# Second layer's edge counts: parts visited in twos, both one-hots on VectorE, ScalarE left with copies

## The reference

```python
h = maximum(layernorm(x), 0)
x_hyp = expmap0(h)
gx = gamma * x_hyp
num = segment_sum(edge_weight[:, None] * gx[dst], src)   # and a denominator beside it
x = x + logmap0(0.5-scaled num / den)
```

## Time and profile before

| | |
|---|---|
| median of 3 runs | 4671.01 us (4664.2 to 4673.88) |
| the profiled execution, its own time | 4658.9 us |
| its span in the trace | 4657.2 us |
| busy in the span: PE, VectorE, ScalarE, POOL | 1625.0, 2841.6, 1721.5, 2023.8 us |
| `blend_and_count` in the trace | about 2100 to 2936 us |

### The profile page before, as it was taken

The page is one execution under the profiler, slowest core; times in us unless marked ns, Lnnn a source line. Parts: engine busy times, 40 slices in busy tenths (PEclk is TensorE's granted clock), DMA queues, the critical chain, the costliest instruction groups (busy, mean ns, idle before and its releaser), DMA issues. The chain is left out here.

```text
span 4657.2 us, 48027 instructions
## 1 busy us (share of the span) xinstructions
PE 1625.0 (35%) x10415; PEld 925.7 (20%) x10415; DVE 2841.6 (61%) x4999; ACT 1721.5 (37%) x4632; POOL 2023.8 (43%) x2740
## 2 busy tenths in 40 slices
PE   3152111100000000002454434222222179899989
PEld 2132111100000000000111101111121069444444
DVE  5837699774677789881354434738697857422131
ACT  1324312102565667331454444325454465111011
POOL 0065788727777710026456663067777540000000
PEclk6576555555555555555665555655555589999999
DMA  3000000016666610002122222168788545777846
GB/s 131 15 19 1 3 1 1 1 57 180 183 182 184 186 42 0 0 18 44 33 62 65 65 64 67 57 184 266 246 261 251 162 128 149 287 240 268 283 162 204
DMA packets 215402, 553.56 MB, mean 119 GB/s; under 512 B 46177, under 2 KB 112411, under 8 KB 214404
## 3 DMA queue, kind: packets, MB, share of 16 engines
q0 software_dynamic: 99984, 272.83, 21.3%
q1 hardware_dynamic: 115188, 278.18, 17.6%
HBM read 485.70 MB, written 65.20 MB: 118 GB/s over the span
## 5 line engine op out<-in xcount | busy, mean ns | idle before, releaser
L2913 PE MATMUL fourth_bank<-fourth_tile,fourth_z 128*128 128x512 f16 (+1 forms) x2800 | 557.2, 360 | 20.1 <-DVEq L3074 10.1
L2272 POOL DMA_INDIRECT heads_got<-rec,heads_slot x416 | 479.2, 1152 | 153.2 <-issue 94.4
L1372 POOL DMA_INDIRECT blend_got<-rec,blend_slot x416 | 403.7, 971 | 291.2 <-DVE second_sums L1412 163.1
L1793 POOL DMA_INDIRECT sum_got<-rec,sum_slot x416 | 440.9, 1060 | 158.7 <-issue 90.2
L1099 POOL DMA_INDIRECT table<-edges_record,edges_place x391 | 419.1, 1072 | 123.5 <-POOL table_pause L260 85.7
L1424 DVE TENSOR_SCALAR blend_mov<-built_iota_low,built_low 128x800 f16 x492 | 218.9, 445 | 377.6 <-issue 226.5
L1492 PE MATMUL blend_count<-blend_mov,blend_stat 128*128 x492 | 220.7, 449 | 459.0 <-issue 302.9
L214 PE MATMUL edges_p_key<-kept_ident,edges_key_row 128*128 128x128 f32 x4 | 1.1, 424 | 1013.6 <-DVEq L176 1013.6
L1879 DVE TENSOR_TENSOR first_y<-first_y,sum_got 128x516 f32 x416 | 291.4, 701 | 80.6 <-issue 34.5
L1465 ACT ACTIVATE blend_gap<-built_iota_ten,built_offset 128x128 f32 x492 | 197.2, 401 | 382.7 <-issue 252.5
L2386 DVE TENSOR_TENSOR third_a_y<-third_a_y,heads_got 128x520 f32 x416 | 288.0, 692 | 60.5 <-issue 36.4
(11 more groups left out here) (679 smaller groups left out, 4694.4 us busy)
## 6 DMA issues: line engine op xcount, KB each, us to landing
fourth_tile<-cs SPq DMA_DIRECT2D x100, 800.0 KB, 4.4
fourth_tile<-ct SPq DMA_DIRECT2D x100, 800.0 KB, 4.4
ct<-blend_cst SPq DMA_DIRECT2D x20, 1000.0 KB
heads_counts<-ct SPq DMA_DIRECT2D x25, 800.0 KB
cs<-heads_flipped SPq DMA_DIRECT2D x25, 800.0 KB
attend_cnt<-ct SPq DMA_DIRECT2D x50, 256.0 KB
sort_low_wide<-low SPq DMA_DIRECT2D x4, 3136.0 KB, 21.7
attend_cnt<-ct SPq DMA_DIRECT2D x25, 288.0 KB
```

The lines of the kernel that those rows point to most:

```text
L1372: pool.indirect_dma_start(got[:, t % KEPT, :], None, rec_dram, bass.IndirectOffsetOnAxis(ap=slot[:, t:t + 1], axis=0)).then_inc(gathered[p ...
L1793: pool.indirect_dma_start(got[:, t % (HELD * PART), :], None, rec_dram, bass.IndirectOffsetOnAxis(ap=slot[:, t:t + 1], axis=0)).then_inc(g ...
L2272: pool.indirect_dma_start(got[:, buf, r, :], None, rec_dram, bass.IndirectOffsetOnAxis(ap=slot[:, t:t + 1], axis=0)).then_inc(gathered[buf ...
L2913: last = pe.matmul(bank[m][:, 0:w], z2[s % 2][:, k, part, :], tile[:, n % RING, at:at + w], start=(k == 0 and part == 0), stop=(k == NB - ...
```

## The change

- The loops go over pairs of parts. `prepare_edges` makes the span of each block even and at least four parts: first part at most `ET - 4`, end rounded up so that the length is even. The tables are two parts longer so that a pair may reach past the last.
- VectorE makes both one-hots, for both parts of a pair: four TENSOR_SCALAR instructions (is_equal), the new ones 128 numbers wide, from 16-bit numbers against `K["offset"]`, which now holds the key minus the start of the group of ten blocks.
- ScalarE has no loop, registers, `gap` or steps for `stat`. It waits for a constant value of `block_done` and copies the block.
- TensorE waits once for a pair and has four matmuls in an iteration. Behind each block comes a matmul of zeros two columns wide that signals `block_done`.
- The rings hold 4 pairs in place of 8 parts.

```diff
-                step(dve.tensor_scalar(K["offset"][:, k, :], K["key"][:, 0:ET], -1.0, float(k * GROUP * P), ALU.mult, ALU.add))
+                step(dve.tensor_scalar(K["offset"][:, k, :], K["key"][:, 0:K["offset"].shape[2]], -float(k * GROUP * P), None, ALU.add))
...
-            step(dve.tensor_scalar(span[:, :, 0], first[:, :], float(ET - 2), None, ALU.min))
-            step(dve.scalar_tensor_tensor(last[:, :], span[:, :, 0], 1.0, last[:, :], ALU.add, ALU.max))
-            step(dve.tensor_scalar(span[:, :, 1], last[:, :], 1.0, None, ALU.add))
+            step(dve.tensor_scalar(span[:, :, 0], first[:, :], float(ET - 4), None, ALU.min))
+            step(dve.scalar_tensor_tensor(last[:, :], span[:, :, 0], 3.0, last[:, :], ALU.add, ALU.max))
+            step(dve.tensor_tensor(last[:, :], last[:, :], span[:, :, 0], ALU.subtract))
+            step(dve.tensor_scalar(last[:, :], last[:, :], 0.5, 0.75, ALU.mult, ALU.add))
+            step(dve.tensor_scalar(last[:, :], last[:, :], ROUND_MAGIC, -ROUND_MAGIC, ALU.add, ALU.add))
+            step(dve.scalar_tensor_tensor(span[:, :, 1], last[:, :], 2.0, span[:, :, 0], ALU.mult, ALU.add))
...
-    RING, BANKS = 8, 2
+    RING, BANKS = 4, 2
-    stat, mov = c.sb("stat", [P, RING, P], BF16), c.sb("mov", [P, RING, IL], BF16)
-    gap = c.sb("gap", [P, RING, P], BF16)
+    stat, mov = c.sb("stat", [P, RING, 2 * P], BF16), c.sb("mov", [P, RING, 2 * IL], BF16)
...
-                with dve.Fori(*tiles_of(dve, tiles, b)) as t:
+                ids = K["iota_ten"][:, b % GROUP * P:(b % GROUP + 1) * P]
+                first, end = tiles_of(dve, tiles, b)
+                with dve.Fori(first, end, step=2) as t:
                     n, at = slot_of(dve, made)
                     dve.wait_ge(slot_free, n + 1)
-                    dve.tensor_scalar(at_slot(mov, at), K["iota_low"][:, :], K["low"][:, bass.ds(t, 1)], None, ALU.is_equal).then_inc(mov_ready, 1)
+                    movs, stats = at_slot(mov, at), at_slot(stat, at)
+                    for k in range(2):
+                        done = dve.tensor_scalar(movs[:, k * IL:(k + 1) * IL], K["iota_low"][:, :], K["low"][:, bass.ds(t, 2)][:, k:k + 1], None, ALU.is_equal)
+                        done = dve.tensor_scalar(stats[:, k * P:(k + 1) * P], ids, K["offset"][:, b // GROUP, bass.ds(t, 2)][:, k:k + 1], None, ALU.is_equal)
+                    done.then_inc(slot_ready, 1)
                     dve.reg_add(made, made, 1)
...
-                act.wait_ge(slot_free, act.snap(visits[b % 2], min_val=1, max_val=BLOCKS * ET) + RING)
+                act.wait_ge(block_done, b + 1)
...
-                with act.Fori(*tiles_of(act, tiles, b)) as t:
-                    n, at = slot_of(act, matched)
-                    act.wait_ge(mov_ready, n + 1)
-                    act.activation(at_slot(gap, at), ids, ACT.Abs, bias=K["offset"][:, b // GROUP, bass.ds(t, 1)]).then_inc(gap_ready, 1)
-                    narrow_of_the_last(n)
-                    act.reg_add(matched, matched, 1)
+                take(b)
...
-                pe.wait_ge(stat_ready, n + 2)
-                pe.matmul(banks[0], at_slot(stat, at), moving[:, 0:IL // 2], start=first, stop=True, skip_group_check=True)
-                pe.matmul(banks[1], at_slot(stat, at), moving[:, IL // 2:IL], start=first, stop=True, skip_group_check=True).then_inc(slot_free, 1)
+                pe.wait_ge(slot_ready, n + 1)
+                movs, stats = at_slot(mov, at), at_slot(stat, at)
+                for k in range(2):
+                    for half in range(2):
+                        done = pe.matmul(banks[half], stats[:, k * P:(k + 1) * P], movs[:, k * IL + half * IL // 2:k * IL + (half + 1) * IL // 2],
+                                         start=first and k == 0, stop=True, skip_group_check=True)
+                done.then_inc(slot_free, 1)
...
-                with pe.Fori(first + 1, end):
+                with pe.Fori(first + 2, end, step=2):
                     visit(banks, False)
+                pe.matmul(banks[1][:, 0:2], K["zero"][:, 0:P], K["zero"][:, 0:2], start=False, stop=True, skip_group_check=True).then_inc(block_done, 1)
```

More of the change, by code:

```diff
@@ L236, in tiles_of @@
     first, end = regs[0][b % GROUP], regs[1][b % GROUP]
-    return eng.snap(first, min_val=0, max_val=ET - 1), eng.snap(end, min_val=1, max_val=ET)
+    return eng.snap(first, min_val=0, max_val=ET - 4), eng.snap(end, min_val=4, max_val=ET + 1)
 class Chain:
@@ L1343, in blend_and_count @@
     gathered = [c.gather_sem(f"gathered{k}") for k in range(PARTS_KEPT)]
-    mov_ready, gap_ready, stat_ready, slot_free = c.sem("mov_ready"), c.sem("gap_ready"), c.sem("stat_ready"), c.sem("slot_free")
+    slot_ready, slot_free, block_done = c.sem("slot_ready"), c.sem("slot_free"), c.sem("block_done")
     sum_free = c.sem("sum_free")
@@ L1433, in _ @@
         def _(act):
-            act.preload_act_table(ACT.Relu)
-            act.copy(at_slot(gap, RING - 1), K["zero"][:, 0:P]).then_inc(gap_ready, 1)
-            matched = counter(act, "matched")
-            visits = [counter(act, f"visits{k}") for k in range(2)]
-            tiles = range_registers(act)
             def take(b):
@@ L1489, in visit @@
                 n, at = slot_of(pe, used)
-                pe.wait_ge(stat_ready, n + 2)
-                moving = at_slot(mov, at)
-                pe.matmul(banks[0], at_slot(stat, at), moving[:, 0:IL // 2], start=first, stop=True, skip_group_check=True)
-                pe.matmul(banks[1], at_slot(stat, at), moving[:, IL // 2:IL], start=first, stop=True, skip_group_check=True).then_inc(slot_free, 1)
+                pe.wait_ge(slot_ready, n + 1)
[5 more added lines that the diff above has]
+                done.then_inc(slot_free, 1)
                 pe.reg_add(used, used, 1)
@@ L1602, in second_layer @@
             K.update(key=ci.sb("key", [P, 512]), low=ci.sb("low", [P, 512]), ones=ci.sb("ones", [P, P]),
-                     iota_low=ci.sb("iota_low", [P, IL], F16), iota_ten=ci.sb("iota_ten", [P, GROUP * P]),
-                     offset=ci.sb("offset", [P, BLOCKS // GROUP, ET]), range=ci.sb("range", [1, 512], I32))
+                     iota_low=ci.sb("iota_low", [P, IL], F16), iota_ten=ci.sb("iota_ten", [P, GROUP * P], F16),
+                     offset=ci.sb("offset", [P, BLOCKS // GROUP, ET + 2]), range=ci.sb("range", [1, 512], I32))
             prepare_edges(nc, src, dst, range_dram, K, h, gam, feat, sums, passed, rec_dram)
```

12 lines of the change are left out of this document (removed).

## The result

The changed kernel takes 4599.1 us (median of 4 runs, 4591.96 to 4614.23) against 4670.17 for the kernel before on the same chip (4 runs). The ratio is 0.9851, 95% interval 0.9816 to 0.9886: 71 us, or 1.5%, faster. The forecast was 4636 us, with a range from 4530 to 4685, which holds the result; the forecast's own range, 4600 to 4660, ends 1 us above it. The gain is twice the 35 us that were forecast.

A forecast was written before the change was run, and what follows sets the result against it. Beside gathers, the slowest engine's control instructions, about 0.7 us each, were taken as the bound. Terms -20, -20 and +9 gave -31, rounded to -35 us: 4636 beside the median 4671.0; range 4530 to 4685, own range 4600 to 4660.

The forecast's parts named there:

- The first stretch: From the first compare to the first add in `blend_and_count`: TensorE sets the pace, first add at 2273 us, -20 us.
- The price forecast: TensorE beside the gathers, before the first add: each control instruction costs 0.71 us, so a pair takes 5.7 us.
- The middle: Blocks while adds and gathers mix, 2302 to 2854 us: VectorE takes 8.5 us a block beside gathers, not 9.1; -20 us.
- the rule: Beside the gathers, the slowest engine's control-instruction count sets the pace; in the middle VectorE's 29 a block take 9.1 us.
- the bound named for TensorE alone: Middle: if TensorE's 21 control instructions for 28 set the pace, 6.8 us a block, 61 blocks fit, -72 us.
- The undisturbed block: A middle block while no gathers run: 4.8 us, from 3.6 + 1.4 x 0.92.
- The last blocks: The last 23 blocks, with no gathers: 4.0 us each against 3.6, +9 us.
- The narrow compare: VectorE's new 128-wide compare: 200 ns each, two in a pair of 1.2 us.
- no term: POOL's gathers: disturbance of only 9 us and more idle time than that, so nothing in the sum.
- That the slots go: Beside the gathers, the 0.7 us slots vanish or shrink as ScalarE leaves: 4425 to 4485 us, half relief 4550; chance 0.17.
- that VectorE's sequencer becomes the bound: Beside the gathers, ten or more control instructions a pair make the kernel slower: +38 us, 4709; chance 0.17.
- No change: Whole stage: 12% more parts eat the shorter loops' gain; start -15, middle -5, end +15, 4666 us; chance 0.12.

The follow-up runs named there:

- the kernel that it is measured against: The changed kernel with POOL waiting for the adds before every gather in place of every eighth: 4547.61 us, ratio 0.9846.

## Why the forecast fell short

**The first stretch.** The forecast was the first add at 2273 us (-20); in the first profile it starts at 2266.3 (-28). That the number is so near is in part luck, for in other profiles of the same instructions the first add follows the first gather 31 to 64 us sooner. The mechanism was as told: near 700 ns for TensorE's address steps, while VectorE's stay short:

```profile
L1431 DVEq FUSED_REGOPS  x24: 16/120/158, 2163.4 to 2235.0; - x24
```

The count was eight control instructions on TensorE and seven on VectorE, as forecast. The price forecast, 8 x 0.71 = 5.7 us a pair, is what the steady part has; the mean of the 80 us is 6.15. From 2120 to 2256 us there are 29 pairs (58 narrow compares) where 24 were expected, since the slow instructions set in gradually: 14 of the 29 pairs fall in the first 43 us. The prediction says that all three engines are busy for under a fifth of this stretch; TensorE's 28.61 us of 136 are 21%, which changes nothing in the argument.

**The middle is the step that failed.** The prediction put it at -20: "if VectorE, now alone, does a block in 8.5, 49 blocks fit beside the gathers", which is -15, and 5 more "since TensorE's wait for ScalarE goes too". It is -43. By the prediction's own division, 521 us less 418 us of gathers are 103, at 4.8 us 21.5 blocks, and the other 56.5 of the 78 took 7.4 us each, not 8.5.

What stood behind the 8.5 was that VectorE's own count stays at 29 a block and sets the pace, and that ScalarE's leaving "frees the chain of jitter, but not VectorE's own count". The count did stay, so the whole -20 was the price of what ScalarE's leaving frees, and this term was too small. Two runs show it. With ScalarE out and single parts VectorE has 34 control instructions a block; by the rule the middle would be some 30 us longer (9.1 x 34 / 29 = 10.7 us a block), and the kernel is 22 us faster. From pairs with ScalarE in to the changed kernel the count goes up from 24 to 29; by the rule the middle would be some 45 us longer, and the kernel is 24 us faster. Taken together ScalarE's leaving is worth an estimated 50 to 70 us beside the gathers, out of which VectorE's added count is paid.

VectorE's count does matter in the middle, as told: two more a pair cost 26 us there and 47 in all. TensorE's doesn't show in the middle (2 us); its 26 us are to be looked for in the first stretch, where the first add comes 33 us later behind the first gather than in the kernel that it is measured against (160.5 us, 127 there), part of which is the scatter of that stretch. So the bound named for TensorE alone (6.8 us, 61 blocks) is nearer to the measured 7.4 than the value taken, but not for its reason. Why ScalarE's loop cost so much is open. It isn't a loop of control instructions on its sequencer (+8 us, inside the intervals), and a relay through it costs some 13 us. ScalarE's activations in the loop are what is left, and they were not tested by themselves. How the 67 us divide between the first stretch and the middle rests on one profile of each kernel; the whole, -71 and -70 us on two chips, doesn't.

The undisturbed block near 4.8 us held: without gathers the adds take 447 us before and 453 after. (Its working, 3.6 + 1.4 x 0.92, is 4.9, and the difference is too small to matter.) But it held as a sum of two things that the prediction didn't name: pairs shorten it (430 us with ScalarE in) and VectorE's extra compares lengthen it.

**The last blocks.** The forecast was +9 us; it is +2. The narrow compare is slower than forecast:

```profile
L1432 DVE TENSOR_SCALAR blend_stat<-built_iota_ten,built_offset x550: 235/249/482, 2112.3 to 2861.8; 128x128 f16 x184
```

249 ns for 200; but it runs into its neighbours. In the timeline of the last blocks a pair of parts begins 1.11 us after the one before:

```profile
2804.05 0.43 DVE L1431 TENSOR_SCALAR blend_mov<-built_iota_low,built_low 128x800 f16 x1
2804.40 0.25 DVE L1432 TENSOR_SCALAR blend_stat<-built_iota_ten,built_offset 128x128 f16 x1
2804.56 0.42 DVE L1431 TENSOR_SCALAR blend_mov<-built_iota_low,built_low 128x800 f16 x1
2804.90 0.25 DVE L1432 TENSOR_SCALAR blend_stat<-built_iota_ten,built_offset 128x128 f16 x1
2805.16 0.43 DVE L1431 TENSOR_SCALAR blend_mov<-built_iota_low,built_low 128x800 f16 x1
```

That is 1.1 us and not 1.2 (the lower end given). With it a block is 2 x 1.1 + 4 x 0.285 + 0.5 = 3.8 us. Behind the start of the last gather 95 adds are left, 22.8 blocks of 4.16 in 84.3 us, 3.7 each; before it was 100 adds, 24.0 blocks in 82.3 us, 3.4 each. Two things make +2 of +9: a block costs 0.3 us more and not 0.4, and there is one block less.

By the Trainium skill ("VectorE: DVE Perf Modes", section on the TRN2 errata) the narrow compare was an estimated 190 ns. The row has 249, and the measurement decides, though in a run of compares the narrow one adds only 0.16 to 0.26 us.

**POOL** is no term, as forecast: the mean gather takes 981 ns, against 971.
The Trainium skill ("SBUF — State Buffer", section on SBUF's two separate sides) warned of two-port instructions that lock GpSimd out; 1,100 of them in place of 492 go with 10 ns more a gather, 4 us in all, where the prediction worked out some 10 us by it. No run shows whether the lock is the cause of these 10 ns.

**The rivals.** That the slots go is refuted: they are there, at the same price, in the changed kernel. That VectorE's sequencer becomes the bound with ten instructions a pair and the kernel slower didn't come about, since it has seven. Its direction was sound, though: with nine a pair 47 of the 70 us are gone; the kernel is still 25 us faster than the one before, where the prediction put the turn at about nine. No change is refuted by the interval.

The forecast's own parts were -20, -20 and +9; measured are -26 (-28 by the clock of the profile), -43 and +2. The sign was right, and so was the way by which the first stretch gains. The size of the middle was off by a factor of two, because what ScalarE's leaving frees there was priced too low.

## What to carry to other kernels

When one engine issues a long chain of transfers and stands still part of the time, find whom it waits for: here its idle time fell by some 80 us, and the kernel's time by 71, while the engines that everybody watches did more work. In loops beside such a chain count the control instructions of each sequencer (branches, address steps, waits), and ask for each stretch which engine is the slowest: two more a pair on TensorE cost time where TensorE was it, two more on VectorE cost nearly twice as much. An engine that leaves the loop can be worth more than the counts say. An edit that loses undisturbed (ScalarE's leaving, +19 us) can win in the place where it runs (-24 us), so its price has to be taken beside the traffic that it will meet. And two profiles of one kernel can differ by tens of microseconds in one stretch (94 to 158 us here), so one profile alone doesn't confirm a term of the sum.

## What the runs showed of the hardware

- Beside gathers 1.33 us apart TensorE's sequencer is slow: a visit with six control instructions takes 4.2 us, a pair with eight 5.7 and one with ten 6.8, about 0.7 us for each (or about 0.5 for each, if weight loads count as well). Without gathers an address step takes 51 ns, and no branch, address step or addition of the stage takes over 352. Why is open; the runs show only that it comes and goes with the gathers and that an idle loop on another engine doesn't make it much worse.
- It doesn't begin with the first gather: in four profiles of the same instructions the first pair over 2.2 us comes 18 to 35 us after it, and the first add comes 94 to 158 us after the first gather.
- Four register additions on one register, one after the other, came out as one more instruction (275 for 275 pairs), four waits as two. A dose has to be read from the trace before a conclusion is drawn from it.
- The kernel before takes 4670 us on one chip and 4620 to 4623 on the others. Ratios carried over from chip to chip (0.9851 and 0.9846), times did not. In the one pair of profiles of the changed kernel from two chips the difference lies in this stage (755 and 712 us).
